# Keys and values of two attentions made earlier and kept in a ring of 16 tiles, with the order of all engines rewritten in seven phases

## The reference

```
x = x + attention0(layernorm(x), ctx)   # 16 heads of size 8, 64 keys, with biases
x = x + experts(layernorm(x))           # 8 experts, each relu(x W1 + b1) W2 + b2, weights of the best 2
x = x + attention1(layernorm(x), ctx)   # 16 heads of size 8, without biases
x = x + cell(layernorm(x))              # c = sigmoid(..)*c + sigmoid(..)*tanh(..), 128 steps in a row
out                                     # tanh(layernorm(x) Wo + c_end Uo + bo)
```

## Time and profile before

| | us |
|---|---|
| median of 3 runs (829.54 to 830.13) | 829.63 |
| the profiled execution | 829.49 |
| its span, first to last instruction | 827.6 |
| PE busy in the span | 809.3 |
| ACT busy | 778.4 |
| DVE busy | 761.7 |
| POOL busy | 682.4 |

### The profile page before, as it was taken

The page is one execution under the profiler, slowest core; times in us unless marked ns, Lnnn a source line. Parts: engine busy times, 40 slices in busy tenths (PEclk is TensorE's granted clock), DMA queues, the critical chain, the costliest instruction groups (busy, mean ns, idle before and its releaser), DMA issues.

```text
span 827.6 us, 43129 instructions
## 1 busy us (share of the span) xinstructions
PE 809.3 (98%) x15312; PEld 732.9 (89%) x15312; DVE 761.7 (92%) x2778; ACT 778.4 (94%) x2490; POOL 682.4 (82%) x1292
## 2 busy tenths in 40 slices
PE   8899999999999999999999999999999999999996
PEld 6698899999999999999999999999999999988784
DVE  6899999999999999999999999999999999999855
ACT  5899999999999999999999999999999999999875
POOL 5888898888888888888888888888888888878634
PEclk9999999999999999999999999999999999999998
DMA  9400000000000000000000000000000000000005
GB/s 342 186 2 4 3 3 4 4 3 4 3 4 3 4 3 3 4 4 4 3 4 4 3 4 4 3 4 3 4 4 3 4 4 3 4 4 4 3 3 204
DMA packets 6973, 17.77 MB, mean 21 GB/s; under 512 B 752, under 2 KB 2288, under 8 KB 6768
## 3 DMA queue, kind: packets, MB, share of 16 engines
q1 hardware_dynamic: 6336, 14.36, 4.6%
q10 hardware_dynamic: 432, 0.68, 0.3%
HBM read 10.84 MB, written 4.19 MB: 18 GB/s over the span
## 4 chain that ended last, share of the span: by engine, by line
PE 90%; DVE 5%; issue 2%; ACT 2%; DMA 1%; POOL 0%; SPq 0%; DVEq 0%; ACTq 0%; POOLq 0%
PE ps L508 14%; PE ps L486 13%; PE ps L421 13%; PE ps L405 8%; PE ps L451 7%; PE ps L582 6%; PE ps L568 5%; PE ps L353 4%; PE ps L368 3%; PE ps L465 3%; PE ps L384 3%; PE ps L432 3%; PE ps L344 1%; PE ps L345 1%; PE ps L521 1%
## 5 line engine op out<-in xcount | busy, mean ns | idle before, releaser
L1701 POOL TENSOR_TENSOR h<-Ex 128x512 f32<-128x512 f32 (+1 forms) x144 | 166.5, 1156 | 42.2 <-issue 39.7
L1230 DVE TENSOR_REDUCE mx<-ps 128x8 f32<-128x512 f32 (+1 forms) x288 | 168.6, 621 | 5.9 <-PE ps L405 5.5
L883 ACT ACTIVATE Ex<-Ex 128x512 f32<-128x512 f32 (+1 forms) x288 | 169.4, 619 | 2.4 <-DVE Ex L1244 2.4
L1340 DVE SCALAR_TENSOR_TENSOR acc<-ps,we,acc 128x128 f32<-128x128 f32 x448 | 150.4, 336 | 21.0 <-PE ps L508 16.1
L1244 DVE TENSOR_TENSOR Ex<-ps,mx 128x512 f32<-128x512 f32 (+1 forms) x288 | 168.4, 622 | 0.3
L894 ACT ACTIVATE ET<-ps 128x512 f32<-128x512 f32 (+1 forms) x288 | 162.9, 575 | 1.3 <-PE ps L421 0.9
L421 PE MATMUL ps<-w,Ex 128*128 128x128 f32 x1024 | 156.6, 274 | 0.7 <-DVE Ex L1244 0.4
L932 ACT ACTIVATE hT<-ps,w 128x128 f32<-128x128 f32 x512 | 148.2, 399 | 1.3 <-PE ps L486 1.2
L486 PE MATMUL ps<-xT,w 128*128 128x128 f32 x1024 | 136.5, 276 | 0.0
L508 PE MATMUL ps<-w,hT 128*128 128x128 f32 x1024 | 134.5, 275 | 0.0
L486 PEld LDWEIGHTS ps<-xT,w 128*128 128x128 f32 x1024 | 124.4, 192 | 3.9 <-issue 3.1
(11 more groups left out here) (110 smaller groups left out, 1796.4 us busy)
## 6 DMA issues: line engine op xcount, KB each, us to landing
cx<-ctx_dram SPq DMA_DIRECT2D x7, 512.0 KB, 13.2
x<-x_dram SPq DMA_DIRECT2D x7, 512.0 KB, 13.9
out_dram<-x SPq DMA_DIRECT2D x14, 256.0 KB, 2.7
w<-weights_dram SPq DMA_DIRECT2D x2, 512.0 KB, 5.6
w<-weights_dram SPq DMA_DIRECT2D x1, 576.0 KB, 8.2
out_dram<-x SPq DMA_DIRECT2D x4, 128.0 KB, 2.6
w<-weights_dram ACTq DMA_DIRECT2D x1, 328.0 KB, 4.9
w<-weights_dram ACTq DMA_DIRECT2D x1, 256.0 KB, 2.8
```

The source lines that it names most:

```text
L883: e.activation(Er, Er, ACT.Exp, scale=SCALE).then_inc(sig(f"E{r}"), 1)
L1230: e.tensor_reduce(mx[:, j % 2, r, 4 * lo:4 * hi], b[:, 256 * lo:256 * hi].rearrange("p (j k) -> p j k", k=64), AX.X, ALU.max).then_inc(sig ...
L1340: m = e.scalar_tensor_tensor(x[:, t, :] if n == 8 else d, b[:, 128 * k:128 * k + 128], we[:, t % 2, n - 1:n], d, ALU.mult, ALU.add)
L1701: e.tensor_tensor(u, v[:, :, :, 0:32], v[:, :, :, 32:64], ALU.add).then_inc(sig("half1"), 1)
```

## The change

Keys and values are made two tiles sooner (LAG kv 1 to -1, kvc 2 to 0). The keys of attention 0 lie in a ring of 8 tiles. The values of attention 0 now go into the ring too, in one copy of 384 columns with those of attention 1, and are spread into Vb from there by a step of its own (vs), four iterations after. The products of weights (BUSY, keep_busy) are left out. There are seven phases in place of four, each with a new order on each engine; the middle phase begins at iteration 7 (before: 12) and ends at 72 (before: 66). Lags of DVE and POOL that differ by one only count the iterations otherwise.

```diff
-RING = 16
+RING, KEYS = 16, 8
-EVEN = 8
-BUSY = {("turnx", 0): (5, 0), ("S", 0): (3, 0), ("bias", 0): (4, 0), ("S", 1): (2, 1), ("q", 2): (3, 1),
-        ("e2", 0): (4, 1), ("S", 2): (1, 1)}
+EVEN = 7
...
-       "kv": 1, "xo0": 10, "re0": 3, "ex3": 4, "ex2": 4, "re1": 3, "kvc": 2, "rT": 5, "sc": 1, "ET2": 4, "gA": 2,
+       "kv": -1, "rT": 5, "re1": 3, "kvc": 0, "gA": 2, "sc": 1, "xo1": 4, "ET1": 4, "qc": 2, "ex1": 3, "xT": 1,
...
-STARTS = (-1, 6, 12, 66)
+STARTS = (-4, 1, 2, 3, 6, 7, 72)
...
-            def keep_busy(name, j):
-
-                n, after_bias = BUSY.get((name, j), (0, 0))
-                if after_bias:
-                    e.wait_ge(sig("bo0"), 1)
-                for _ in range(n):
-                    e.matmul(lstm[:, 128:256], wkv[:, WK, :], wkv[:, WK1, :], start=True, stop=True, skip_group_check=True)
...
+                if t >= KEYS:
+                    e.wait_ge(sig("K0"), t - KEYS + 1)
+                e.activation(kT[:, t % KEYS, :], b[:, 0:128], ACT.Identity, bias=col[:, BK:BK + 1]).then_inc(sig("kT"), 1)
+                if t >= RING:
+                    e.wait_ge(sig("V1"), t - RING + 1)
+                    e.wait_ge(sig("K1"), t - RING + 1)
+                e.activation(kvr[:, t % RING, :], b[:, 128:512], ACT.Copy).then_inc(sig("kvc"), 1)
+
+            def spread_values(i):
+                t = i - LAG["vs"]
+                if not on(t):
+                    return
+                e.wait_ge(sig("kvc"), t + 1)
+                if t == 0:
                     e.wait_ge(sig("cleared"), 1)
-                if t >= 2:
-                    e.wait_ge(sig("K0"), t - 1)
-                e.activation(kT[:, t % 2, :], b[:, 0:128], ACT.Identity, bias=col[:, BK:BK + 1]).then_inc(sig("kT"), 1)
                 if t >= 4:
                     e.wait_ge(sig("pv"), t - 3)
                 for h in range(2):
-                    src = b[64 * h:64 * h + 64, 128:256].rearrange("p (g two d) -> p g two d", two=2, d=8)
+                    src = kvr[64 * h:64 * h + 64, t % RING, 0:128].rearrange("p (g two d) -> p g two d", two=2, d=8)
                     dst = Vb[64 * h:64 * h + 64, 1, t % 4, :, :, 0:4:3, 8 * h:8 * h + 8]
-                    e.activation(dst.rearrange("p s j w d -> p (s j) w d"), src, ACT.Copy)
-                if t >= RING:
-                    e.wait_ge(sig("V1"), t - RING + 1)
-                    e.wait_ge(sig("K1"), t - RING + 1)
-                e.activation(kv1[:, t % RING, :], b[:, 256:512], ACT.Copy).then_inc(sig("kvc"), 1)
+                    m = e.activation(dst.rearrange("p s j w d -> p (s j) w d"), src, ACT.Copy)
+                m.then_inc(sig("vs"), 1)
```

More of the change, by code:

```diff
@@ L126, in due @@
 def due(i, name):
-    ahead = AHEAD.get(name, (0, 0, 0, 0))
+    ahead = AHEAD.get(name, (0, 0, 0, 0, 0, 0, 0))
     done = max(r + ahead[phase(r)] for r in range(i - 48, i))
@@ L614, in tensor_program @@
                     gate(r)
+                for r in due(i, "rt"):
+                    turn_r(r)
+                for r in due(i, "pv"):
+                    values(r)
+                for r in due(i, "sB"):
+                    step(r, 1)
+                for r in due(i, "e3"):
+                    turn_e(r, 3)
                 for r in due(i, "sA"):
                     step(r, 0)
+                for r in due(i, "xin"):
+                    cell_inputs(r)
+                for r in due(i, "p"):
+                    project(r)
@@ L617, in tensor_program @@
                 for r in due(i, "e2"):
                     turn_e(r, 2)
+                for r in due(i, "h1"):
+                    hidden(r, 1)
+            for i in range(STARTS[3], STARTS[4]):
+                for r in due(i, "h1"):
+                    hidden(r, 1)
+                for r in due(i, "e0"):
+                    turn_e(r, 0)
+                for r in due(i, "turnw"):
+                    turn_w(r)
+                for r in due(i, "e3"):
+                    turn_e(r, 3)
+                for r in due(i, "S"):
+                    scores(r)
+                for r in due(i, "sB"):
+                    step(r, 1)
+                for r in due(i, "rt"):
+                    turn_r(r)
+                for r in due(i, "kv"):
+                    keys_values(r)
+                for r in due(i, "pv"):
+                    values(r)
+                for r in due(i, "turnx"):
+                    turn_x(r)
+                for r in due(i, "e1"):
+                    turn_e(r, 1)
+                for r in due(i, "e2"):
+                    turn_e(r, 2)
+                for r in due(i, "xin"):
+                    cell_inputs(r)
+                for r in due(i, "y1"):
+                    experts(r, 1)
+                for r in due(i, "p"):
+                    project(r)
+                for r in due(i, "wx0"):
+                    out_inputs(r, 0)
+                for r in due(i, "wx1"):
+                    out_inputs(r, 1)
+                for r in due(i, "q"):
+                    query(r)
@@ L619, in tensor_program @@
                 for r in due(i, "y0"):
                     experts(r, 0)
+                for r in due(i, "sA"):
+                    step(r, 0)
+                for r in due(i, "gate"):
+                    gate(r)
+                for r in due(i, "h0"):
+                    hidden(r, 0)
+                for r in due(i, "yb"):
+                    expert_bias(r)
+            for i in range(STARTS[4], STARTS[5]):
+                for r in due(i, "wx1"):
+                    out_inputs(r, 1)
+                for r in due(i, "h0"):
+                    hidden(r, 0)
+                for r in due(i, "pv"):
+                    values(r)
+                for r in due(i, "wx0"):
+                    out_inputs(r, 0)
+                for r in due(i, "yb"):
+                    expert_bias(r)
+                for r in due(i, "turnx"):
+                    turn_x(r)
+                for r in due(i, "kv"):
+                    keys_values(r)
+                for r in due(i, "e1"):
+                    turn_e(r, 1)
+                for r in due(i, "sA"):
+                    step(r, 0)
+                for r in due(i, "q"):
+                    query(r)
+                for r in due(i, "rt"):
+                    turn_r(r)
+                for r in due(i, "e2"):
+                    turn_e(r, 2)
+                for r in due(i, "gate"):
+                    gate(r)
+                for r in due(i, "y1"):
+                    experts(r, 1)
+                for r in due(i, "sB"):
+                    step(r, 1)
+                for r in due(i, "h1"):
+                    hidden(r, 1)
+                for r in due(i, "e3"):
+                    turn_e(r, 3)
@@ L1017, in scalar_program @@
+            for i in range(STARTS[5], STARTS[6]):
                 if i == 8:
@@ new lines, in scalar_program @@
+                for r in due(i, "vs"):
+                    spread_values(r)
+            for i in range(STARTS[6], LAST):
+                for r in due(i, "qc"):
+                    query(r)
+                for r in due(i, "ET2"):
+                    turn_e(r, 2)
+                for r in due(i, "weT"):
+                    turn_w(r)
+                for r in due(i, "re1"):
+                    relus(r, 1)
+                for r in due(i, "xo0"):
+                    out_inputs(r, 0)
+                for r in due(i, "gB"):
+                    gates(r, 1)
+                for r in due(i, "ET1"):
+                    turn_e(r, 1)
+                for r in due(i, "xT"):
+                    turn_x(r)
@@ L1809, in gpsimd_program @@
                     keys(r, 1)
-                for r in due(i, "km1"):
-                    keys(r, 0)
+            for i in range(STARTS[6], LAST):
+                for r in due(i, "km0"):
+                    keys(r, 1)
+                for r in due(i, "wep"):
+                    gate_pieces(r)
                 for r in due(i, "xb"):
```

1282 lines of the change are left out of this document (846 added, 436 removed), and 132 rows, old and new, of tables (AHEAD, LAG, USES).

## The result

The changed kernel takes 822.44 us (median of 4 runs, 822.29 to 823.31); the kernel before, measured beside it, 829.59. The ratio is 0.9917 with a 95% interval of 0.9902 to 0.9933: faster by 7.15 us. Forecast were 826.0, with a range of 823 to 831. The profiled run took 822.29, its span is 820.2 us, 7.4 less than before.

What follows compares the result with a forecast made beforehand. The prediction took PE, busy 809.3 of 827.6 us, to bound the kernel. Its terms, +0 - 1.4 - 1.0 - 1.2 = -3.6 us, gave 825.9 from the profiled 829.49, or 826.0 for the median; range 823 to 831.

Steps and rivals of the forecast that it cites:

- Term 1: Middle, scores of item 12 to 63: PE's instructions stay the same, so 11.885 us per iteration stays; change 0.
- The part on ACT: Middle: larger copy and two spreads from SBUF add 0.09 to 0.24 us per iteration, inside ACT's slack of 0.32.
- Term 2: Start, to the sixth scores: without products of weights and waits for bo0, later scores come sooner; -1.4 us.
- S0's +0.4: Start: first scores come at 9.99 in place of 9.57, behind the second x's turning, copy and query product.
- The bound by DVE: Start, first to sixth scores: gain at most 3.6 us, since DVE has no more idle time to give.
- Term 3: Way into the middle, sixth scores to item 12: middle's lists from iteration 7 recover PE's lost time; -1.0 us.
- Term 4: Last two full iterations, S61 to S63: no keys and values made, but DVE limits the gain; -1.2 us.
- The drain's own order: Drain: new orders from iteration 72 in place of 66; taken as 0, with 1.0 us either side.
- ACT as the bound: Rival, middle: spreads from SBUF exceed ACT's slack, 834 us, slower; chance 0.16 including another stall in the middle.
- The clock: Rival, start: without the products PE's clock falls to 1.2 GHz, costing 2.1 us, time 828.0; chance 0.14.
- DVE ate nothing: Rival, fill and drain: DVE, nearly as busy as PE, eats the gain, leaving -1.0, 828.6 us; chance 0.18.

Runs made afterwards that it cites:

- e1: The changed kernel with all four engines following the old orders in iterations 12 to 61: 826.93 us.
- e11: The kernel before with only the ring added (copy of 384 columns, spread into Vb from SBUF): 830.13 us, ratio 1.0004.
- e12: The kernel before with its drain order beginning at iteration 70 in place of 66: 830.27 us.
- e3: The kernel before with the 22 products of weights and their waits for bo0 left out: 830.11 us, ratio 1.0004.
- e8: The kernel before with only the ten products of weights behind bvo and their waits for bo0 left out: 829.62 us.
- e13: The kernel before with ring, eight tiles of keys and sets two tiles sooner, but old orders and the 22 products of weights kept: 832.74 us.
- e14: The kernel before with ring, eight tiles of keys and sets two tiles sooner, old orders, without the 22 products of weights: 831.71 us.
- e7: The changed kernel with keys and values three tiles sooner from iteration 6 on, that iteration making two sets: 826.72 us.
- e2: The changed kernel with the 22 products of weights and their waits for bo0 put back: 825.40 us.
- e6: The changed kernel with the old orders on DVE and POOL alone in iterations 14 to 61: 822.58 us.
- e5: The changed kernel with the old orders on PE and ACT alone in iterations 14 to 61: 918.89 us.
- e9: The changed kernel with DVE's eight pieces of work on the experts' bias made one iteration later: 824.05 us.

## Why the prediction was wrong

**Term 1 (0, measured -1.72) is the step that failed.** It said of the middle "so its 11.885 us stay if no other engine overtakes it", and looked only for what could make it slower. Of the 3.8 us between forecast and measured span, 1.7 lie here, the largest part. The kernel before did not run at 11.885: my own division of the window gave 11.91, and seven iterations of 12.05 to 12.19 stood in the trace. DVE's seven single delays, 1.7 us together, reached PE in the old order; the new order takes such delays without PE feeling them, and e1 brings the long intervals back one by one. The part on ACT was right: 48 ns for a spread (46 forecast), 134 for the copy (145), 0.23 in all inside a slack of 0.32, and e11 shows an unchanged interval with most of the slack gone.

The range had a slip of its own. It says that the bounds of terms 2 to 4 end together at -7.2, 822.4; the bounds given are 3.6, 3.4 and 2.0, together 9.0, which is 820.6. The measured 822.44 lies within them, and below the stated 823.

**Term 2 (-1.4, measured -2.5 at S5) had the wrong cause.** S0's +0.4 was right in size (+0.32), with some luck: S0 came at 9.00 to 9.57 in three profiled runs of the old opening (before, e11, e12) and at 9.41 to 10.23 in six of the new. But the gain was ascribed to the products left out and their wait for bo0. In the kernel before these are worth nothing either way (e3, e8), and sooner sets in the old order lose (e13, e14): S0 to S5 takes 28.7 to 29.5 us in every kernel with the old fill and 25.9 to 28.3 in those with the new one but for e7. By elimination the new order is the gain, alone or together with the sooner sets that it was made for; it is also what makes the products a loss of 3.0 when put back (e2). The size, 2.5, is that of a fast run: where the clock fell (e6) the gain from S0 to S5 was 0.8. The bound by DVE (3.6) held.

**Term 3 (-1.0, measured -1.40)** was nearly right in size, and 1.05 of it lies in S9 to S12, where e1 with the old order took 1.60 more. The reason given, a PE that loses about 0.5 in each such interval, fits only roughly: the three intervals are 0.24, 0.61 and 0.20 shorter, and PE's visible idle time from S5 to S12 fell by 0.5 (1.62 to 1.14). What the rest was is not shown.

**Term 4 (-1.2; S61 to the end measured -1.78).** The two iterations were found, their size was not: "there DVE takes over ... 11.37" gave 0.5 each, measured were 0.78 and 0.52 (11.10 and 11.25). DVE did 79 instructions there for 82 before (22.00 us for 22.77), and 88 for 83 behind S71 (25.41 for 23.78): it put work off to the tail instead of holding PE. A share of busy time over the middle is no floor for two iterations. In the old order the gain would have been 0.06 and 0.14, by PE's wait for the chain (e13). The drain's own order, set to 0 with 1.0 either way, gave -1.42 and +0.95.

**The rivals.** ACT as the bound did not come (e11). The clock did not fall in the profiled run of the changed kernel. That was in part luck: with the same instructions in the opening it fell in e5, e6 and e7 behind S1, and it falls in e9 and in the old order without all its products (e3, e8, e14). The rival's price of 2.1 us is near what e6 shows, whose clock fell: its profiled run took 824.59, for 822.29 of after. DVE ate nothing: the middle and fill of the new order have room beside it.

## What to carry to other kernels

A pipeline whose busiest engine is busy all the time can still be late: list the intervals from one iteration to the next and look at those that are longer than the median, since a chain without slack turns each single delay of another engine into time, and also swallows work that is taken away. Ask of a filler (here products that keep the clock up) what stands in its place in the new order before crediting its removal. And judge one engine's new list only with the others': of two mixtures of old and new lists one cost 2 us an iteration (e5) and the other nothing (e6). And a profile is one run: with one and the same opening the clock held in three profiled runs here and fell in three others, so look at several before reading a gain from one.

## What the runs showed of the hardware

DVE started up to 0.32 us late seven times in some 500 us with nothing to wait for, at places multiples of 128 instructions apart in its stream (one more or less), and at the same numbers of its stream in different kernels (all seven in before, e1, e11 and e14, five of them in after); the cause is open.

By the length of its rows PE ran at its lower rate at the start, until 4.4 us in before and until about 7.0 in after and e1 (two rows of the first set take 0.38 or 0.64 us, the 8 rows ahead of them 3.38 to 3.78), though the granted clock of 4.75:7.00 in after reads 1.00. S0 doesn't follow from it: 9.57 in before, 9.00 in e12, whose rate rose at 4.65.

An operation of DVE of 0.2 to 0.3 us with its data in SBUF took 0.86 to 1.08 beside one of POOL that had begun first (before, e1, e5, e6, e7, e9). In a fill that waits at that point this is some 0.8 us of S1, and in four of these runs (e5, e6, e7, e9) the clock fell behind it.
